# Macaron block on one core: routing gates moved into the token rows, first-layer results added by accumulating DMAs

## The reference

```
x = x + 0.5 * ffn(layernorm(x))
x = x + attn(layernorm(x))
x = x + 0.5 * ffn(layernorm(x))

def ffn(h):
    probs  = softmax(h @ gate_W.T)                    # 8 experts
    gates  = the two largest probs of a token, else 0
    out_e  = (silu(h @ w1_e) * (h @ w3_e)) @ w2_e     # hidden width 512
    routed = sum over e of gates_e * out_e
    shared = sum over 8 small experts (width 64) / 8
    return 0.5 * shared + 0.5 * routed

def attn(h):
    q, k, v = split(rms_norm(h) @ w_qkv.T); q, k = rms_norm(q), rms_norm(k)
    w  = exp(k);  y = cumsum(w * v) / (cumsum(w) + 1e-6) * sigmoid(q)
    u, g = split(y @ w_swiglu.T)
    return h + (u * silu(g)) @ w_out.T
```

## Time and profile before

| | |
|---|---|
| three runs | 768.84, 772.85, 773.11 us; median 772.85 |
| the profiled execution | 769.99 us, of which 768.2 us are the span of the profile |
| busy share of the span | PE 89%, DVE 58%, POOL 55%, ACT 47% |
| chain of work that ended last | PE 72%, DVE 14%, ACT 5%, issue 4%, DMA 2%, POOL 2% |

### The profile page before, as it was taken

One profiled execution on the slowest core, in us unless ns is written; L12 is line 12 of the kernel. 1 busy time (PEld: TensorE's weight loads), 2 busy tenths in 40 slices (PEclk: granted clock), 3 DMA queues, 4 the chain that ended last, 5 costly groups with the idle time before them and its releaser, 6 DMA issues.

```text
span 768.2 us, 12865 instructions
## 1 busy us (share of the span) xinstructions
PE 683.8 (89%) x4282; PEld 582.3 (76%) x4282; DVE 443.5 (58%) x1089; ACT 361.7 (47%) x921; POOL 418.9 (55%) x491
## 2 busy tenths in 40 slices
PE   4878859999999999956886777999999999999995
PEld 3766758888888888834654574888888888888883
DVE  6678864434434444447999986874444443443338
ACT  2659413444444444458874536652444444444442
POOL 6600584567667664459897515016366766765330
PEclk9989979999999999989999997999999999999998
DMA  9800001111111111041110110001011111111039
GB/s 305 307 1 0 2 24 36 38 45 50 45 47 50 45 46 33 32 116 42 42 29 28 29 42 14 1 5 52 18 48 51 46 45 49 47 48 38 29 109 244
DMA packets 45023, 43.76 MB, mean 57 GB/s; under 512 B 5985, under 2 KB 39777, under 8 KB 44577
## 3 DMA queue, kind: packets, MB, share of 16 engines
q1 hardware_dynamic: 35872, 24.32, 10.3%
q0 software_dynamic: 9088, 18.63, 8.7%
HBM read 27.33 MB, written 15.60 MB: 56 GB/s over the span
## 4 chain that ended last, share of the span: by engine, by line
PE 72%; DVE 14%; ACT 5%; issue 4%; DMA 2%; POOL 2%; SPq 1%; POOLq 0%; DVEq 0%; ACTq 0%
PE psY L1467 16%; PE psH L1450 8%; PE psG L1308 5%; PE psU L1308 5%; PE psU L1310 5%; PE psU L1309 5%; PE psG L1310 5%; PE psG L1309 5%; PE psH L1379 5%; PE psT L1407 2%; DVE XN L733 2%; DVE hs L743 1%; DVE rec L1043 1%; POOL results L636 1%; DVE ln_stats L720 1%
## 5 line engine op out<-in xcount | busy, mean ns | idle before, releaser
L636 POOL DMA_INDIRECT results<-yout,target x142 | 139.7, 984 | 119.4 <-DVE yout L947 83.3
L743 DVE TENSOR_TENSOR hr<-silu,psU 128x512 f32<-128x512 f32 x142 | 97.6, 687 | 173.3 <-PE psU L1310 171.6
L621 POOL DMA_INDIRECT rows<-tokens,source x142 | 137.0, 965 | 94.6 <-DVE source L891 42.9
L1194 ACT ACTIVATE silu<-psG 128x512 f32<-128x512 f32 x142 | 85.1, 599 | 162.7 <-PE psG L1310 162.5
L1467 PE MATMUL psY<-W,hT 128*128 x1120 | 148.0, 275 | 0.0
L1467 PEld LDWEIGHTS psY<-W,hT 128*128 128x128 f32 x1120 | 136.1, 192 | 0.0
L1187 ACT ACTIVATE hT<-psH 128x512 f32<-128x512 f32 x142 | 84.8, 597 | 77.2 <-PE psH L1450 77.2
L1450 PEld LDWEIGHTS psH<-ident,hr 128*128 128x128 f32 x568 | 70.6, 141 | 19.6
L1450 PE MATMUL psH<-ident,hr 128*128 128x128 f32 x568 | 85.1, 272 | 0.0
L1122 ACT ACTIVATE silu<-psG 128x512 f32<-128x512 f32 x64 | 37.9, 593 | 70.4 <-PE psG L1310 55.4
L743 DVE TENSOR_TENSOR hs<-silu,psU 128x512 f32<-128x512 f32 x64 | 43.6, 684 | 45.9 <-PE psU L1310 38.1
(11 more groups left out here) (187 smaller groups left out, 1268.8 us busy)
## 6 DMA issues: line engine op xcount, KB each, us to landing
W<-w_e SPq DMA_DIRECT2D x3, 2048.0 KB, 13.7
tokens<-XN SPq DMA_DIRECT2D x16, 256.0 KB, 3.6
Y<-results SPq DMA_DIRECT2D x32, 128.0 KB, 2.2
YF<-results SPq DMA_DIRECT2D x16, 256.0 KB, 5.1
rows<-tokens,source POOLq DMA_INDIRECT x142, 2.6
results<-yout,target POOLq DMA_INDIRECT x142, 2.3
X<-x SPq DMA_DIRECT2D x8, 256.0 KB, 5.4
out<-X SPq DMA_DIRECT2D x8, 256.0 KB, 2.6
```

Source lines behind the costliest of these rows:

```text
L621: pool.indirect_dma_start(rows[:, g % RING, t, :], None, tokens, bass.IndirectOffsetOnAxis(ap=source[:, tile:tile + 1], axis=0))\
L636: pool.indirect_dma_start(results, bass.IndirectOffsetOnAxis(ap=target[:, tile:tile + 1], axis=0), yout[:, g % 2, t, :], None).then_inc(y_ ...
L743: dve.tensor_tensor(hidden, silu[:, s.u % 2, :], psU[:, s.u % 2, :], ALU.mult).then_inc(h_done, 1)
L1194: act.activation(silu[:, s.u % 2, :], psG[:, s.u % 2, :], ACT.Silu).then_inc(silu_done, 1)
```

## The change

- A row of `tokens` becomes 130 floats (`ROW`): the two gates of the token stand behind its 128 values. DVE writes the gates into XN; `keep_tokens` waits for them (`gates_done`) before it writes the first chunk. The routed gather brings both gates of each row; a table `is_choice` says for each slot which of the two counts, and DVE forms `gate` from them, two small instructions for each group of four tiles in `copy_xT`. The multiply of the hidden tile takes `gate` as a scalar (`scalar_tensor_tensor`), so the results leave the routed stretch already weighted. A group's buffer is refilled after `xT_done` and no longer after `xT_psum`.
- The rows of `results` are ordered so that the rows that one partition reads lie next to each other (`(k p i) d`, was `(k i p) d`). `table` works this out and makes `is_choice`: ten instructions in place of seven.
- After layer 0 the load into Y, ACT's scaling and POOL's additions are gone. POOL waits until all results are sent and issues twelve DMAs that add from DRAM to X in SBUF, for six groups of tiles (`ADDED`: 2, 2, 4, 8, 8, 8 tiles) and two choices. The second of a group waits until the first has landed. Six are issued ahead of the attention stages, six at POOL's steps 0 to 4 ahead of that step's stages. `at_statistics` waits for its group.
- All attention stages come two steps earlier, as the two stages in front are gone; `TURNED_STEP` and `SCORED_STEP` move with them. `LN_STEPS`, by its own formula, becomes steps 16, 16, 17, 18, 19, 20, 21 for chunks 0 to 6; it was 16, 16, 17, 18, 19, 21, 23.
- After layer 1, `add_half` is one plain addition of 128x512 in place of four scaled ones, `scale_half` is gone, and PE sums YF as it landed.

```diff
+ROW = D + TOPK
-POOL_STAGES = [("qkv_rsqrt", 5), ("residual", 5), ("at_rsqrt", 3), ("mean_square", 4), ("add_routed", 1)]
+POOL_STAGES = [("qkv_rsqrt", 3), ("residual", 3), ("at_rsqrt", 1), ("mean_square", 2)]
...
+ADDED = ((0, 2), (2, 2), (4, 4), (8, 8), (16, 8), (24, 8))
+ADD_FIRST = ((0, 0), (1, 0), (0, 1), (2, 0), (1, 1), (2, 1))
+ADD_STEPS = {0: ((3, 0),), 1: ((3, 1), (4, 0)), 2: ((4, 1),), 3: ((5, 0),), 4: ((5, 1),)}
...
-        results_v = results[0:TOPK * NT, :].rearrange("(k i p) d -> p k i d", k=TOPK, p=P)
+        results_v = results[0:TOPK * NT, :].rearrange("(k p i) d -> p k i d", k=TOPK, p=P)
...
                 def keep_tokens(s):
+                    sp.wait_ge(gates_done, l + 1)
...
+            def add_results(n, k):
+                first, count = ADDED[n]
+                tiles = slice(first, first + count)
+                if k == 0:
+                    pool.wait_ge(sh_added, FRONT[0] if first + count <= FRONT[0] * CH else CHUNKS)
+                else:
+                    pool.wait_ge(y_added[n], 16)
+                pool.dma_start(X[:, tiles, :], results_v[:, k, tiles, :], accum_op=ALU.add).then_inc(y_added[n], 16)
...
-                        pool.wait_ge(xT_psum, GROUPS * l + g - RING + 1)
+                        pool.wait_ge(xT_done, GROUPS * l + g - RING + 1)
...
                 if l == 0:
+                    for p in range(2):
+                        pool.wait_ge(y_sent[p], sent(0, p, GROUPS // 2))
+                    for n, k in ADD_FIRST:
+                        add_results(n, k)
+                    def between(step):
                         def run():
+                            for n, k in ADD_STEPS.get(step, ()):
+                                add_results(n, k)
+                            if step < POOL_END:
+                                for c in LN_STEPS.get(step, ()):
+                                    scale_ln(1, Step.of(c, 2))
...
-                dve.tensor_scalar(gates[:, 0, :], row_b[:, :], 0.25, None, ALU.mult)
+                dve.tensor_scalar(XN[:, :, D], row_b[:, :], 0.25, None, ALU.mult)
...
-                    route.then(dve.tensor_copy(spare[:, :], place))
-                    route.then(dve.scalar_tensor_tensor(found[:, :], rest, float(P), spare[:, :], ALU.mult, ALU.add))
-                    route.then(dve.scalar_tensor_tensor(spare[:, :], found[:, :], 0.5, own_row[:, :],
+                    route.then(dve.tensor_copy(spare, place))
+                    route.then(dve.scalar_tensor_tensor(found[:, :], rest, float(P), spare, ALU.mult, ALU.add))
+                    route.then(dve.scalar_tensor_tensor(spare, spare, float(TILES), rest, ALU.mult, ALU.add))
+                    route.then(dve.tensor_scalar(other, found[:, :], float(NT + P) - 0.5, None, ALU.is_ge))
+                    route.then(dve.scalar_tensor_tensor(spare, other, float(NT - TILES), spare, ALU.mult, ALU.add))
+                    route.then(dve.scalar_tensor_tensor(target[:, :], found[:, :], 0.5, own_row[:, :],
                                                         ALU.is_lt, ALU.mult))
-                    dve.scalar_tensor_tensor(target[:, :], found[:, :], float(-P), spare[:, :], ALU.add, ALU.add)\
+                    dve.scalar_tensor_tensor(target[:, :], spare, -1.0, target[:, :], ALU.add, ALU.add)\
                        .then_inc(table_link, 1)
                     dve.wait_ge(table_link, l + 1)
-                    route.then(dve.tensor_scalar(spare[:, :], found[:, :], float(NT + P) - 0.5, float(-NT),
-                                                 ALU.is_ge, ALU.mult))
                     route.then(dve.tensor_scalar(found[:, :], found[:, :], float(-P), 0.0, ALU.add, ALU.max))
-                    dve.tensor_tensor(source[:, :], found[:, :], spare[:, :], ALU.add).then_inc(table_done, 1)
+                    dve.scalar_tensor_tensor(source[:, :], other, float(-NT), found[:, :], ALU.mult, ALU.add)\
+                       .then_inc(table_done, 1)
+                    dve.tensor_scalar(first, other, -1.0, 1.0, ALU.mult, ALU.add).then_inc(choices_made, 1)
...
+                    dve.tensor_tensor(gate_parts[:, par, 0:n, :], rows[:, g % RING, 0:n, D:ROW],
+                    dve.tensor_reduce(gate[:, par, 0:n], gate_parts[:, par, 0:n, :], X_AXIS, ALU.add)
...
+                    dve.scalar_tensor_tensor(hr[:, s.u % 2, :], silu[:, s.u % 2, :],
+                                             gate[:, s.over(GT) % 2, s.u % GT:s.u % GT + 1],
+                                             psU[:, s.u % 2, :], ALU.mult, ALU.mult).then_inc(h_done, 1)
...
-                        for t in range(c * CH, (c + 1) * CH):
-                            i = dve.scalar_tensor_tensor(X[:, t, :], YF[:, k, t, :], gates[:, k, t:t + 1], X[:, t, :],
+                        i = dve.tensor_tensor(xs, xs, YF[:, k, c * CH:(c + 1) * CH, :], ALU.add)
...
-                    dve.wait_ge(routed_added, s.i + 1)
+                    dve.wait_ge(y_added[max(n for n, (first, _) in enumerate(ADDED) if first <= s.i * TB)],
+                                16 * TOPK)
```

More of the change, by code:

```diff
@@ L171, in sem @@
             return ctx.enter_context(nc.semaphore(name))
-        tokens = nc.dram_tensor("tokens", [NT, D], fp32, kind="Internal").ap()
+        tokens = nc.dram_tensor("tokens", [NT, ROW], fp32, kind="Internal").ap()
         results = nc.dram_tensor("results", [(TOPK * TILES + TILES_R) * P, D], fp32, kind="Internal").ap()
@@ L240, in macaron @@
         pos_part = sb("pos_part", [P, 2, TOPK * TILES])
-        gates = sb("gates", [P, TOPK, TILES])
+        is_choice = sb("is_choice", [P, TOPK, TILES_R])
+        gate_parts = sb("gate_parts", [P, 2, GT, TOPK])
+        gate = sb("gate", [P, 2, GT])
         found = sb("found", [P, TILES_R])
-        spare = sb("spare", [P, TILES_R])
         source = sb("source", [P, TILES_R], i32)
@@ L317, in macaron @@
              ("ha", [P, 2, TB * P], fp32)],
-            [("rows", [P, RING, GT, D], fp32)],
+            [("rows", [P, RING, GT, ROW], fp32)],
             [("XNTL", [P, NT], fp32r), ("XNTH", [P, NT], fp32r)])
@@ L397, in macaron @@
         y_sent = [sem(f"y_sent{p}") for p in range(2)]
-        y_in = [sem(f"y_in{p}") for p in range(4)]
+        y_added = [sem(f"y_added{n}") for n in range(len(ADDED))]
         yf_in = [sem(f"yf_in{c}") for c in range(CHUNKS)]
-        y_scaled = sem("y_scaled")
-        add_link = sem("add_link")
         last_link = sem("last_link")
-        last_scaled = sem("last_scaled")
         last_added = sem("last_added")
@@ L688, in _ @@
                 if l == 0:
-                    stages = {"qkv_rsqrt": qkv_rsqrt, "add_routed": add_routed, "residual": residual,
+                    for p in range(2):
+                        pool.wait_ge(y_sent[p], sent(0, p, GROUPS // 2))
+                    for n, k in ADD_FIRST:
+                        add_results(n, k)
+                    stages = {"qkv_rsqrt": qkv_rsqrt, "residual": residual,
                               "at_rsqrt": at_rsqrt, "mean_square": mean_square}
-                    def scale_ahead(chunks):
+                    def between(step):
                         def run():
-                            for c in chunks:
-                                scale_ln(1, Step.of(c, 2))
+                            for n, k in ADD_STEPS.get(step, ()):
[3 more added lines that the diff above has]
+                                    scale_ln(1, Step.of(c, 2))
                         return run
                     pipelined(pool, [(stages[n], d) for n, d in POOL_STAGES], BATCHES, 4, straight=True,
-                              at={k: scale_ahead(chunks) for k, chunks in LN_STEPS.items() if k < POOL_END})
+                              at={k: between(k) for k in range(POOL_END)})
         @block.vector
@@ L1406, in transpose_rows @@
                     for t in range(min(GT, RUN - g * GT)):
[L1407 removed]
+                        i = pe.transpose(psT[:, t * P:(t + 1) * P], rows[:, g % RING, t, 0:D], ident[:, :])
                     i.then_inc(xT_psum, 1)
```

109 lines of the change are left out of this document (46 added, 63 removed).

## The result

| | median of the runs (us) | lowest to highest | ratio to before, 95% interval |
|---|---|---|---|
| before, beside it | 772.98 (4 runs) | 768.84 to 773.88 | |
| after | 789.97 (4 runs) | 786.34 to 791.24 | 1.0223 (1.0195 to 1.0251) |

The changed kernel is 17 us slower. Its profiled execution took 791.24 us with a span of 789.5, so the two profiles differ by 21.3 us of span, more than the medians, as the profile before is of one of its faster executions. I split that at points which both traces have; the third column is what the prediction gave the stretch.

What follows compares the result with a forecast made beforehand. Bounds: PE in the routed stretch, DVE and POOL at layer 0's table, DVE with PE close behind in attention. Terms 3.4 + 7.9 - 2.4 - 3.0 - 2.8 = +3.1 us; forecast 775 us, range 766 to 788.

Steps and rivals of the forecast that it cites:

- the price of an adding DMA: Start of attention: 128, 256 and 512 KB added into X were taken to land in 2.6, 3.5 and 5.2 us.
- the upper end of 8.4: Start of attention: dearest price considered for a 512 KB adding DMA, in us, taken from YF loads in a full queue.
- the prediction's own sign: Start of attention: wrong in size if 512 KB land outside 4 to 6.5 us; wrong in kind if POOL is not held.
- the first rival: Start of attention: dear adding DMAs make POOL's waits hold its square roots; over 1% slower, up to 791 us; chance 0.27.
- The start: Start of attention: POOL's waits on adding DMAs delay the square roots, +7.9 us; +5.2 at lower prices, +19 at upper.
- the table: Layer 0's table: more DVE instructions each wait for a POOL instruction, +3.4 us, between 2.3 and 6.9.
- tokens and gathers: Token writes and routed gathers: later writes and longer rows cost nothing; the third rival said +10 us, 785, chance 0.04.
- the step of the steady part: Steady attention: a step falls from 5.69 to 5.42 us without ACT's scaling, -2.4 us over nine steps.
- fewer steps by themselves: Start of attention: two steps fewer bring nothing; the second rival said two whole steps gained, 762 us, chance 0.13.
- The last part of attention: Attention's end with layer 1's normalising: part of DVE's idle time is won, -3.0 us, between 0 and -4.4.
- The end: End of layer 1: six single additions on the path replace four-instruction ones, 0.46 us each, -2.8 us.
- that case: End of layer 1: YF comes faster in pieces of 2 KB than of 512 bytes, up to 1.4 us more gained.

Runs made afterwards that it cites:

- e1_plain: The changed kernel with its twelve adding DMAs into X as plain copies, same shapes, order and waits; 774.01 us, ratio 1.0013.
- e4: The changed kernel with POOL's low halves of the expert weights formed after layer 0's table, not beside it; 786.67 us, ratio 1.0181.
- e3: The changed kernel without adding DMAs: SP loads into Y, POOL adds, gates still in the rows, one stage less deep than before; 768.24 us, ratio 0.9934.
- e7: e3 with all attention stages but the routed addition one step later, so as deep as the kernel before; 768.55 us, ratio 0.9963.
- e5: e3 with layer 0's first gathers ahead of the low halves of the expert weights, and these behind the table; 759.10 us, ratio 0.9856.

## Why the prediction was wrong

**The step that failed** is a term of the sum, the price of an adding DMA: "I take what it is if each byte moves twice [...]: 2.6, 3.5 and 5.2, nearer to the lower end because these DMAs run almost alone." Measured were 3.5, 4.8 and 6.9 us in the median. And they did not run alone: POOL issues them in pairs, so that the two on which the square roots waited took 8.72 and 9.05, beyond even the upper end of 8.4. The row that I took for that end, the YF load in a full queue, was the better neighbour. I priced each DMA by itself, while the order written out by hand puts two in flight together; that the pairing makes up the 2 us beyond the median was not tested. By the prediction's own sign, over 6.5 us for 512 KB, it was wrong in size and not in kind. e1_plain bears this out: its copies cost 2.7, 3.1 and 4.4 us, near the 2.6, 3.5 and 5.2 of my sum, and it took 774.01 us, near my 775. An issue, on the other hand, takes POOL 0.55 to 0.9 us and not 1.27.

**What followed from it** was foreseen: POOL's order holds the square roots, the first rival puts the total over 1% slower from about 6.5 us for 512 KB on, and its time of 791 is what the runs gave. It had a chance of 0.27, and my range ended at 788, short of it. The start came out at +22.7 against its +19. `at_fac` of batch 2 is 18.6 us late (46.9 us after the last scatter, 28.3 before), about those 19; the rest is then nearly all in the 3.9 us that I estimate above for PE's lower clock, for which the prediction had no term.

**Right:** the table (+3.4 predicted; `hs` is 3.6 later, and 2.9 are left at the last scatter), with the cause of DVE's waits shown by e4; nothing for tokens and gathers (the DMAs of `tokens` now take 6.3 us each, 3.6 before, and the start of the routed stretch moved by no more than the table did, 3.7 us); nothing for DVE's longer multiply (748 ns in the mean, beside busy PE); the step of the steady part (5.42 predicted, 5.39 measured, and in e3, where POOL still adds and ACT scales nothing, 5.39 to 5.50 from 375.13 on, so ACT's scaling had been most of the 0.3 us); nothing to speak of for fewer steps by themselves (e7, for one step of the two).

**Too large a gain** stood in two places. The last part of attention gave 1.9 and not 3.0. The end gave 0.9 and not 2.8: I counted six additions on the path at 0.46 us each, and behind PE's last `out_shared` the sums on PE took their place. YF as a whole did come faster in pieces of 2 KB, but not the load that DVE waits for first; for that case the prediction had -1.4. And 0.7 us were lost in layer 1, which I had put at nothing; the cause stays open.

The sum of the table in the first section, 21.3 against 3.1, is 18.2 off: 14.8 from the start, 1.9 from the end, 1.1 from the last part of attention, and the rest small.

## What to carry to other kernels

A wait for a DMA in an engine's queue costs whatever stands behind it in that queue. So price such a DMA as it is issued, with those in flight beside it, and put the wait a step or more after the issue, behind the short work that everything else needs: together with smaller groups first this was worth 18 us here. A stage that a change makes slightly longer may be stalled already: the table cost the change 3 us, and mending it on both sides, DVE's wait for POOL and PE's for the gathers, gave 6 to 9 (e5 against e3). Where loads are issued faster, the time to landing of one of them says little: look at the rate, and at the load that is waited for first. A wait halved at the end of a kernel is worth nothing when the output's transfers end it.

## What the runs showed of the hardware

- Adding 128, 256 and 512 KB from DRAM to SBUF by a DMA took 3.5, 4.8 and 6.9 us; the same as plain copies, from the same queue, 2.7, 3.1 and 4.4. About 0.55 us behind another of its kind a 512 KB addition took 8.72 and 9.05.
- PE's granted clock stood at 0.50 from 376 to 384 us, after PE had worked 2.13 of the 6.00 us before; four matmuls took 2.93 us there and 1.56 from 389 on.
- Loads of 256 KB in pieces of 2 KB moved at 399 GB/s, in pieces of 512 bytes at 293, though one load took 6.0 us to land in place of 5.1.
- Beside POOL's instructions of 2.35 us a DVE instruction of 128x72 with two inputs in SBUF took 2.28 us, alone 0.23; one of 128x8 took 9.14 beside them (e5), 0.16 without them.
